# Scores in groups of three tiles with one exponential of 1536 columns each, in a two-layer transformer on one core

## The reference

```python
scores = jnp.einsum('bhqd,bhkd->bhqk', qh, kh) * scale
a = jax.nn.softmax(scores, axis=-1)
return jnp.einsum('bhqk,bhkd->bhqd', a, v)
```

## Time and profile before

| | |
|---|---|
| median of 3 runs | 846.43 us (844.07 to 846.95) |
| profiled execution | 843.49 us, span 841.7 us |
| granted TensorE clock, mean | 0.993 |
| TensorE busy | 773.7 us, 92% |
| ScalarE busy | 763.4 us, 91% |
| VectorE busy | 543.6 us, 65% |
| exponentials (L732) | 768, busy 725.9 us |
| values (L904) | 3072 products, busy 410.0 us |
| scores (L885) | 1024 and 512 products, busy 130.2 and 64.8 us |

### The profile page before, as it was taken

One profiled execution on the slowest core, in us unless ns is written; L12 is line 12 of the kernel. 1 busy time (PEld: TensorE's weight loads), 2 busy tenths in 40 slices (PEclk: granted clock), 3 DMA queues, 4 the chain that ended last, 5 costly groups with the idle time before them and its releaser, 6 DMA issues.

```text
span 841.7 us, 17809 instructions
## 1 busy us (share of the span) xinstructions
PE 773.7 (92%) x6751; PEld 269.5 (32%) x6751; DVE 543.6 (65%) x1200; ACT 763.4 (91%) x856; POOL 36.2 (4%) x56
## 2 busy tenths in 40 slices
PE   8888889999999899998999999998998899999997
PEld 6122223332433233332332223332242333423332
DVE  7877884867674686656685666747768376377322
ACT  3979989989899998999989999999988899899985
POOL 4100000000000100001000010000000000000000
PEclk9999999999999999999999999999999999999998
DMA  3827347602538025650357315390254603302500
GB/s 104 179 44 147 94 99 181 90 1 77 138 94 115 14 77 138 136 73 14 125 134 123 42 52 146 81 150 8 94 133 112 96 2 124 78 2 78 137 13 14
DMA packets 42452, 74.88 MB, mean 89 GB/s; under 512 B 6552, under 2 KB 8216, under 8 KB 42360
## 3 DMA queue, kind: packets, MB, share of 16 engines
q1 hardware_dynamic: 40560, 68.12, 37.5%
q0 software_dynamic: 1744, 5.44, 2.1%
q10 hardware_dynamic: 56, 0.10, 0.0%
HBM read 36.84 MB, written 35.65 MB: 86 GB/s over the span
## 4 chain that ended last, share of the span: by engine, by line
PE 54%; ACT 25%; DVE 10%; issue 8%; DMA 2%; SPq 1%; DVEq 0%; ACTq 0%
ACT probs L732 25%; PE ps_pv L904 20%; PE ps_s L885 14%; PE ps_misc L753 7%; PE ps_misc L757 6%; PE ps_misc L758 4%; PE ps_misc L746 2%; DMA q_ab<-shifts 1%; DMA parts_dram<-qk_parts 1%; DVE pv_sb L1389 1%; ACT ff_out L687 0%; DVE qk_parts L1191 0%; DVE qk_parts L1193 0%; SPq L469 0%; DVE h_lo L1143 0%
## 5 line engine op out<-in xcount | busy, mean ns | idle before, releaser
L732 ACT ACTIVATE probs<-ps_s 128x1024 f32<-128x1024 f32 x768 | 725.9, 1046 | 42.7 <-PE ps_s L885 41.2
L904 PE MATMUL ps_pv<-probs,v_aug 128*32 128x512 f32 x3072 | 410.0, 606 | 9.9 <-DVE pv_sb L1389 4.4
L885 PE MATMUL ps_s<-q_ab,k_ab 18*128 18x512 f32 x1024 | 130.2, 497 | 25.7 <-ACT probs L732 22.2
L885 PEld LDWEIGHTS ps_s<-q_ab,k_ab 18*128 18x128 f32 x1024 | 49.4, 182 | 186.0 <-ACT probs L732 151.9
L904 PEld LDWEIGHTS ps_pv<-probs,v_aug 128*32 128x32 f32 x3072 | 61.6, 108 | 105.8 <-issue 73.1
L1141 DVE CAST h_hi<-ff_out 128x512 fp32r<-128x512 f32 x64 | 27.3, 427 | 101.0 <-ACT ff_out L685 99.6
L757 PE MATMUL ps_misc<-h_hi,k_w 128*128 128x512 f32 x192 | 86.3, 449 | 0.3
L885 PE MATMUL ps_s<-q_c,k_c 32*128 32x512 f32 x512 | 64.8, 495 | 21.1 <-ACT probs L732 20.9
L1389 DVE STREAM_TRANSPOSE pv_sb<-ps_pv 128x512 f32<-128x512 f32 x48 | 34.4, 716 | 74.5 <-PE ps_pv L904 73.0
L758 PE MATMUL ps_misc<-h_lo,k_w 128*128 128x512 f32 x192 | 76.5, 398 | 0.0
L757 PEld LDWEIGHTS ps_misc<-h_hi,k_w 128*128 128x128 f32 x192 | 36.1, 188 | 87.0 <-issue 52.8
(11 more groups left out here) (167 smaller groups left out, 558.5 us busy)
## 6 DMA issues: line engine op xcount, KB each, us to landing
parts_dram<-qk_parts SPq DMA_DIRECT2D x94, 256.0 KB, 3.7
parts_dram<-qk_parts SPq DMA_DIRECT2D x16, 512.0 KB, 2.8
q_c<-parts_dram SPq DMA_DIRECT2D x32, 256.0 KB, 4.9
k_c<-parts_dram SPq DMA_DIRECT2D x32, 256.0 KB, 7.2
q_ab<-parts_dram SPq DMA_DIRECT2D x60, 128.0 KB, 4.8
k_ab<-parts_dram SPq DMA_DIRECT2D x60, 128.0 KB, 6.0
x_ring<-in_L_attn_x_dram POOLq DMA_DIRECT2D x7, 256.0 KB, 3.0
out_dram<-x_ring POOLq DMA_DIRECT2D x7, 256.0 KB, 2.9
```

The costliest lines, as they stand in the source:

```text
L732: nc.scalar.activation(probs[:, U.slot(s), 2 * half:2 * half + 2], ps_s[:, 2 * pair:2 * pair + 2], ACT.Exp, bias=-SCALE[1] * BOUND[1] if U ...
L885: ins = nc.tensor.matmul(ps_s[:, bank, :], k[row:row + n, slot, c * P:(c + 1) * P], q[row:row + n, slot, :], start=True, stop=True)
L904: ins = nc.tensor.matmul(ps_pv[32 * j:32 * j + 32, :], v_aug[:, U.v, c, a:a + 32], probs[:, U.slot(s), j, :], start=c == 0 and not odd, st ...
```

## The change

The 1536 score tiles (384 steps of four) are numbered through and taken in groups of three (`Triple`), 512 groups. A group has three banks of `ps_s`, one half or the other in turn, and one exponential of 1536 columns; where a group holds tiles of both layers, the exponential is cut in two, since scale and bias differ. `probs` becomes a ring of 12 tiles (as large as before). `scores_made` and `exps_made` count groups; `triples_for(n)` gives the groups that hold the first n tiles. Group t's scores wait for t - 1 exponentials.

`ahead(S)` says how many groups are made by step S: the rounded-up third of 4S + 2. So of three steps, two bring one group and one (S = 2, 5, 8, ...) brings two, next to each other, ahead of its values. Values and jobs keep their places: the step's scores, the values of step S-2, the jobs. `operands_there` holds the waits for operands, now taken by the group with a unit's first tile.

```diff
+PROBS = 12
+TRIPLES = UNITS * STEPS * 4 // 3
+class Triple:
+    def __init__(self, t):
+        self.t = t
+        self.banks = 3 * (t % 2)
+        self.probs = 3 * t % PROBS
+        self.tiles = [Tile(3 * t + i) for i in range(3)]
+    def runs(self):
+        layers = [tile.U.layer for tile in self.tiles]
+        cut = next((i for i in range(1, 3) if layers[i] != layers[0]), 3)
+        return [(a, b, layers[a]) for a, b in ((0, cut), (cut, 3)) if a < b]
+def triples_for(tiles):
+    return -(-tiles // 3)
+def ahead(S):
+    return min(triples_for(4 * S + 2), TRIPLES)
...
-        probs = sb("probs", [P, 3, 4, N], F32)
+        probs = sb("probs", [P, PROBS, N], F32)
...
-                sp.wait_ge(scores_made, 2 * U.first_step)
+                sp.wait_ge(scores_made, triples_for(4 * U.first_step))
...
-            pool.wait_ge(scores_made, 2 * STEPS)
+            pool.wait_ge(scores_made, triples_for(4 * STEPS))
...
+            def exp(tr):
+                wait(act, pv_made, (3 * tr.t + 2 - PROBS) // 4 + 1)
+                act.wait_ge(scores_made, tr.t + 1)
+                for a, b, layer in tr.runs():
+                    ins = nc.scalar.activation(probs[:, tr.probs + a:tr.probs + b], ps_s[:, tr.banks + a:tr.banks + b], ACT.Exp,
+                                               bias=-SCALE[1] * BOUND[1] if layer == 1 else 0.0, scale=SCALE[layer])
+                ins.then_inc(exps_made, 1)
...
-                    for half in range(2):
-                        pair = U.pairs(s)[half]
-                        wait(act, pv_made, S - 2)
-                        act.wait_ge(scores_made, 2 * S + half + 1)
-                        nc.scalar.activation(probs[:, U.slot(s), 2 * half:2 * half + 2], ps_s[:, 2 * pair:2 * pair + 2], ACT.Exp,
-                                             bias=-SCALE[1] * BOUND[1] if U.layer == 1 else 0.0, scale=SCALE[U.layer]).then_inc(exps_made, 1)
+                    for t in range(done, ahead(STEPS * u + s)):
+                        exp(Triple(t))
+                    done = ahead(STEPS * u + s)
...
-            def scores(U, s):
-                wait(pe, exps_made, 2 * S - 1)
-                for j in range(4):
+            def scores(tr):
+                for tile in tr.tiles:
+                    operands_there(tile)
+                wait(pe, exps_made, tr.t - 1)
+                for i, tile in enumerate(tr.tiles):
+                    row, slot = TILE_ROWS * j, slot0 + g
+                    ins = nc.tensor.matmul(ps_s[:, tr.banks + i, :], k[row:row + n, slot, c * P:(c + 1) * P], q[row:row + n, slot, :],
+                                           start=True, stop=True)
+                ins.then_inc(scores_made, 1)
...
-                pe.wait_ge(exps_made, 2 * S + 2)
+                pe.wait_ge(exps_made, triples_for(4 * S + 4))
...
-                    scores(U, s)
+                    S = STEPS * u + s
+                    for t in range(done, ahead(S)):
+                        scores(Triple(t))
+                    done = ahead(S)
```

More of the change, by code:

```diff
@@ L206, in __init__, with exact_first @@
         self.times = self.b // 2 if self.layer == 1 else self.b
[L208 to L212, removed]
+class Triple:
[8 more added lines that the diff above has]
+        return [(a, b, layers[a]) for a, b in ((0, cut), (cut, 3)) if a < b]
+class Tile:
+    def __init__(self, n):
+        S, self.j = n // 4, n % 4
+        self.U, self.s = Unit(S // STEPS), S % STEPS
+def triples_for(tiles):
+    return -(-tiles // 3)
+def ahead(S):
+    return min(triples_for(4 * S + 2), TRIPLES)
+def exact_first(u, s):
+    items = TABLE[u].get(s, [])
+    return bool(items) and items[0][0] in ("exact0", "exact1")
 def values_free(layer, b):
@@ L722, in _ @@
                 nc.scalar.copy(qk_parts[:, i, 0, :], bank_of((name, 0))).then_inc(first_hi, 1)
+            done = 0
             for u in range(UNITS):
-                U = Unit(u)
                 for s in range(STEPS):
-                    S = U.first_step + s
-                    for half in range(2):
-                        pair = U.pairs(s)[half]
-                        wait(act, pv_made, S - 2)
-                        act.wait_ge(scores_made, 2 * S + half + 1)
-                        nc.scalar.activation(probs[:, U.slot(s), 2 * half:2 * half + 2], ps_s[:, 2 * pair:2 * pair + 2], ACT.Exp,
-                                             bias=-SCALE[1] * BOUND[1] if U.layer == 1 else 0.0, scale=SCALE[U.layer]).then_inc(exps_made, 1)
+                    for t in range(done, ahead(STEPS * u + s)):
+                        exp(Triple(t))
+                    done = ahead(STEPS * u + s)
                     if (u, s) == (1, 0):
@@ L738, in _ @@
                         job(item)
+            for t in range(done, TRIPLES):
+                exp(Triple(t))
             for item in EPILOGUE:
@@ L872, in exact_max, with operands_there @@
                     pe.sem_inc(gen_made[layer], GEN_MADE[layer])
-            def scores(U, s):
[L876 to L879, removed]
-                wait(pe, exps_made, 2 * S - 1)
-                for j in range(4):
[L882 to L885, removed]
+            def operands_there(tile):
+                U, s = tile.U, tile.s
+                if tile.j != 0:
+                    return
+                if U.u == 0:
+                    if s == 0:
+                        warm(WARM_AGAIN)
+                        wait_taken(pe, ("fast", 0, "k", 0))
+                        pe.wait_ge(shift_loaded["A"], SHIFTED)
+                    elif s == 4:
+                        wait_taken(pe, ("fast", 0, "k", 1))
+                    elif s == 8:
+                        pe.wait_ge(qk_loaded["A"], loaded(U))
+                        pe.wait_ge(first_k_loaded, 16 * TILES)
+                        pe.wait_ge(k_ones_loaded, K_ONES)
+                elif s == 0:
+                    pe.wait_ge(qk_loaded[U.stack], loaded(U))
+                    if U.layer == 0:
+                        pe.wait_ge(shift_loaded[U.stack], SHIFTED * (U.times + 1))
@@ new lines, in scores @@
+            def scores(tr):
[3 more added lines that the diff above has]
+                for i, tile in enumerate(tr.tiles):
+                    U, j = tile.U, tile.j
+                    g, c = tile.s // 4, tile.s % 4
+                    q, k, slot0, _ = operands(U)
+                    n = ROWS[U.layer] + (PARTS if U.layer == 0 else 0)
+                    row, slot = TILE_ROWS * j, slot0 + g
+                    ins = nc.tensor.matmul(ps_s[:, tr.banks + i, :], k[row:row + n, slot, c * P:(c + 1) * P], q[row:row + n, slot, :],
@@ L886, in scores @@
                                            start=True, stop=True)
-                    if j % 2 == 1:
-                        ins.then_inc(scores_made, 1)
+                ins.then_inc(scores_made, 1)
             def pv(U, s):
@@ L903, in pv @@
                     a = (4 * g + j) * VHEAD + (0 if odd else VW)
-                    ins = nc.tensor.matmul(ps_pv[32 * j:32 * j + 32, :], v_aug[:, U.v, c, a:a + 32], probs[:, U.slot(s), j, :],
+                    ins = nc.tensor.matmul(ps_pv[32 * j:32 * j + 32, :], v_aug[:, U.v, c, a:a + 32], probs[:, (4 * S + j) % PROBS, :],
                                            start=c == 0 and not odd, stop=c == 3 and odd == 1)
@@ L929, in _ @@
                 for s in range(STEPS):
[L930 to L945, removed]
-                    scores(U, s)
+                    S = STEPS * u + s
+                    for t in range(done, ahead(S)):
+                        scores(Triple(t))
+                    done = ahead(S)
                     items = TABLE[u].get(s, [])
-                    exact = items and items[0][0] in ("exact0", "exact1")
-                    holds = heads_within(int(items[0][0][-1]), items[0][1]) if exact else None
+                    holds = heads_within(int(items[0][0][-1]), items[0][1]) if exact_first(u, s) else None
                     if s >= 2:
```

## The result

The changed kernel took 867.88 us (865.03 to 870.25, 4 runs) against 846.69 us (844.07 to 847.12, 4 runs): ratio 1.0256, 95% interval 1.0215 to 1.0296. The forecast was 865 us. The profiled execution took 869.15 us, its span was 867.4, 25.7 more than the profiled one of before; between the medians lie 21.2 us.

The account below looks back on a forecast made before the run. TensorE and ScalarE bound the kernel in a ring, neither alone. Profiled 843.5 + 18 (cycles) + 0.5 (operand waits) = 862, scaled to the runs' median 865 us; range 835 to 884, the forecast's own 855 to 880.

Parts of the forecast that it names:

- Exponentials: On ScalarE, 1536 columns take 1.34 us start to start, lasting 1.47; 0.10 us saved per three-step cycle, 13 us over 128.
- The fourth block, x: On TensorE, price of the score block next to another in each three-step cycle: 0.33 us, between 0.23 and 0.44.
- The ring: TensorE and ScalarE waiting on each other, scores in two three-bank buffers instead of three two-bank; cycles sum to +17.8 us.
- quiet cycles: Three steps without a job on TensorE, 12 of 128: ScalarE-bound, 5.46 to 5.36 us, -0.10 each.
- one-job cycles: Three steps with one TensorE job, 54 of 128: 5.81 to 5.84 us, +0.03 each.
- two-job cycles: Three steps with two TensorE jobs: in neighbouring steps (24) +0.41 us each, with a step between (17) +0.06.
- three-job cycles: Three steps with three TensorE jobs, 20 of them: pure TensorE, 6.90 to 7.23 us, +0.33 each.
- b: Second group of a cycle's adjacent pair of score groups; the values were said to wait for no later exponential than it.
- What moves besides: Outside the ring: operand waits at unit ends +0.5 us; ReLUs behind long exponentials up to +6, left to the range.
- The first: Rival, faster: longer exponential keeps ScalarE busy through jobs; one-job cycles save 24 us, about -13, 833 us; chance 0.2.
- The second: Rival, no visible change: fourth block's price near zero and lead from quiet cycles pays the rest, 847 us; chance 0.08.
- The third: Rival, much slower: TensorE bound everywhere, b a block of its own, 0.44 us per non-quiet cycle, +51, 895 us; chance 0.08.

## Why the prediction was right

Direction and cause held: the fourth block of scores costs TensorE more than the shorter exponentials save. The size, 865 forecast and 867.9 measured, is in part luck, since errors in the terms cancelled. By its steps:

- *Exponentials.* Pitch 1.34, duration 1.458 us mean for the whole ones (1.47 forecast), 522 of them, busy time down 10.8 us (13). The Trainium skill's figures (ScalarE: Activation LUTs, What ACT_TABLE_LOAD costs) would have given an estimate of 1.37 us from start to start (1536 columns at the page's 0.833 ns and 93 ns left of its fixed part); the trace's fixed part held.
- *The fourth block, x.* Taken as 0.33, measured 0.23, the low end, which is what one product costs behind another in the same array shape. With it the sum was +14, so the term was 3.7 us too large. The rule of the Trainium skill (TensorE: Matmul & The Clock Gate, Part 3) that a weight load overlaps running products only in another row group would have made it 0.44; the same part also lets a load into the background weight buffer go ahead of running products. The pair at 592.97, in which two of three strips were still in use and all six loads lie within 0.29 us, disagrees with the rule and fits the second sentence.
- *The ring.* Here the sum was right with its parts wrong. Over 118 cycles, leaving out the stretch around the half clock, quiet cycles cost +0.22 us where -0.10 stood, one-job cycles +0.18 (+0.03), two-job cycles +0.08 (+0.26 in the mean of both kinds), three-job cycles +0.31 (+0.33). Carried to all cycles, that is +2.6, +9.7, +3.3 and +6.2 us where the sum had -1.2, +1.6, +10.8 and +6.6: 22 against 18. Quiet and one-job cycles were 12 us too low together, two-job cycles 7.5 too high; that these offset each other is luck. A likely reason, which no run tests: I had let each kind of cycle repeat itself; in the table they alternate, and lateness from a job is paid in the next, quieter cycle. Quiet cycles of 5.36 us are not the rule: in each turn of the loop the one quiet cycle takes 5.84 us where it took 5.34.
- *A missing term.* "The values themselves wait for no later exponential than b does" is true and I took it for "don't wait". As long as b stands ahead of them it hides their wait. Four experiments missed by 6 to 19 us, and in each of them the values wait 22 to 30 us for exponentials. In the changed kernel it is 1.7 us, so the forecast itself didn't suffer from it.
- *What moves besides.* The waits for the loads of `q_ab` fell from 2.6 to 0.8 us instead of costing 0.5. ReLUs waited for their product 19.4 us instead of 11.3. The cost feared was another, TensorE waiting for the ReLU, up to 6 us: its products waited for `ff_out` 0.9 us in all, and 0.7 before. So that term was next to nothing.
- *Rivals.* The first (longer exponential absorbs the jobs) fell: ScalarE's idle time rose. Its own sum is 1 us off (-24 + 16 is -8, not -9), which moves nothing. The second fell: the adjacent block costs 0.23 us, not near zero. The third fell as well: the adjacent block is cheap in 65 pairs, and only 21 of its 51 us came. TensorE's waits for exponentials fell by 12 us, not to nothing.
- Some 4 of the profiled execution's 25.7 us came from a half clock that the forecast didn't have in it. The quickest of the four runs, 865.03 us, lies 21 us above the quickest of before.

## What to carry to other kernels

When two engines are both near 90% busy, a change that saves fixed cost on one and adds a block of work to the other is priced by the block: here 11 us of ScalarE against 128 blocks of 0.23 us of TensorE, and the second decided in either ring. Shorten one engine's work alone to a harmless size and time both kernels so; the difference shows what the other engine's work can explain. Then take the new work itself away: the two answers need not add up, and the gap between them is the coupling. And when an instruction that waits is moved or removed, look at who behind it waits for the same event.

## What the runs showed of the hardware

- A second group of three score products, two of whose strips are still in use, puts the next block off by 0.23 us; a group that stands alone takes 0.43 until the values start.
- TensorE's clock fell to half during a wait of 1.47 us for 13.7 us, in another kernel (split exponentials) 0.2 us after one of 1.39 us for 3.4 us, and stayed full through a wait of 1.90 us at the same values in a third.
